# Edge softmax on Trainium2: the second and third bf16 part read as upper halves of fp32 rests, the first part cast by ScalarE

## The reference

```python
w_m = (efeat @ W_msg + b_msg).reshape(E, 16, -1)
w_a = (efeat @ W_attn + b_attn).reshape(E, 16, -1)
h_src = feat[src][:, :, None]
e1 = w_m * h_src
e2 = w_a * h_src
seg_max = jax.ops.segment_max(e2, dst, num_segments=N)
ex = jnp.exp(e2 - seg_max[dst])
denom = jax.ops.segment_sum(ex, dst, num_segments=N)
ft = jax.ops.segment_sum(e1 * (ex / denom[dst]), dst, num_segments=N)
return ft.sum(axis=1)
```

## Time and profile before

| what | before |
|---|---|
| median of three runs | 5007.65 us |
| lowest and highest run | 5004.14 and 5008.03 us |
| the profiled execution | 4998.83 us |
| its span in the profile | 4997.0 us |
| busy in that span: PE, DVE, ACT, POOL | 3246.4, 3526.0, 1651.5, 3172.5 us |
| starts of the softmax's first product (L1403) and last ratio (L1441) | 41.10 and 1365.97 us |
| instructions of the split | 49 of each of the five |

### The profile page before, as it was taken

How to read it: one execution, slowest core, us unless ns; L and a number is a source line. 1 busy time by engine, 2 the same in 40 slices (tenths; PEclk the granted TensorE clock), 3 DMA queues, 4 the chain that set the end, 5 groups by cost and what they waited for, 6 DMA issues and landing times. The chain is left out here.

```text
span 4997.0 us, 55839 instructions
## 1 busy us (share of the span) xinstructions
PE 3246.4 (65%) x12357; PEld 2401.4 (48%) x12357; DVE 3526.0 (71%) x5827; ACT 1651.5 (33%) x4258; POOL 3172.5 (63%) x2763
## 2 busy tenths in 40 slices
PE   7999999999824444427998344453444447777686
PEld 3444444444424444426887334443434326777542
DVE  8999999999976555525888456644556764555688
ACT  4565665666532111103444111131111232222144
POOL 4777777777637888887888777707776007777000
PEclk9999999999976555558999556685566655655698
DMA  4111111111043333432121100040000230000022
GB/s 111 41 44 41 46 44 40 44 45 42 22 127 68 61 59 59 60 37 53 50 54 48 17 7 7 7 110 8 7 7 6 75 81 7 7 7 7 8 66 66
DMA packets 373578, 211.63 MB, mean 42 GB/s; under 512 B 105770, under 2 KB 343662, under 8 KB 373442
## 3 DMA queue, kind: packets, MB, share of 16 engines
q1 hardware_dynamic: 254162, 190.55, 13.3%
q0 software_dynamic: 119296, 19.68, 6.7%
HBM read 151.70 MB, written 58.34 MB: 42 GB/s over the span
## 5 line engine op out<-in xcount | busy, mean ns | idle before, releaser
L697 POOL DMA_INDIRECT extra<-x_t,srci x784 | 763.0, 973 | 503.9 <-issue 490.9
L1161 PE MATMUL ps<-arena 128*128 128x128 f32 x2976 | 662.6, 412 | 635.7 <-DVE arena L1623 583.8
L1161 PEld LDWEIGHTS ps<-arena 128*128 128x128 f32 x2976 | 615.8, 315 | 671.8 <-issue 665.1
L1065 PE MATMUL ps<-edge_in,wl 17*128 17x512 f32 x784 | 701.8, 1072 | 17.6 <-DVE arena L1415 13.5
L684 POOL DMA_INDIRECT sums<-cmb,sidx x392 | 610.9, 1558 | 134.4 <-issue 120.7
L646 POOL DMA_INDIRECT xg<-in_x,xidx x392 | 466.8, 1191 | 259.0 <-DVE xp L1276 139.4
L633 POOL DMA_INDIRECT ft_t<-fts,fidx x392 | 507.3, 1294 | 144.2 <-issue 120.1
L1623 DVE TENSOR_TENSOR arena<-jmask,ps 128x1024 f32<-128x1024 f32 (+1 forms) x186 | 227.0, 1220 | 502.0 <-ACT ps L899 494.9
L1640 DVE TENSOR_TENSOR arena<-arena,ps 128x128 f32 x1488 | 426.1, 286 | 179.9 <-DVE arena L1640 17.3
L697 POOL DMA_INDIRECT extra<-h_t,srci x392 | 369.9, 944 | 241.5 <-issue 241.5
L1104 PE MATMUL ps<-arena 128*128 128x128 f32 x992 | 223.9, 417 | 450.3 <-DVE arena L1491 354.1
(11 more groups left out here) (204 smaller groups left out, 5935.4 us busy)
## 6 DMA issues: line engine op xcount, KB each, us to landing
edge_in<-far_row SPq DMA_DIRECT2D x98, 256.0 KB
ain<-in_src_row SPq DMA_DIRECT2D x56, 448.0 KB, 3.7
sums<-zero SPq DMA_DIRECT2D x132, 144.0 KB, 3.0
arena<-rel_t SPq DMA_DIRECT2D x63, 256.0 KB, 4.0
x_t<-yout SPq DMA_DIRECT2D x28, 448.0 KB, 3.3
xin<-x_t SPq DMA_DIRECT2D x28, 448.0 KB, 4.4
extra<-x_t,srci POOLq DMA_INDIRECT x784, 2.3
ain<-x_t SPq DMA_DIRECT2D x28, 448.0 KB, 4.8
```

The lines of the kernel that those rows point to most:

```text
L697: pool.indirect_dma_start(dy[:, t, :], None, table, bass.IndirectOffsetOnAxis(ap=srci[:, t:t + 1], axis=0)).then_inc(d_gathered[n % QUEUE] ...
L1065: last = pe.matmul(ps[k][:, h * ET:(h + 1) * ET], wl[:, (k * CH + h) * P:(k * CH + h + 1) * P], eft[b][:, :], start=True, stop=True)
L1161: last = pe.matmul(slot_sums(k, n)[:, j * P:(j + 1) * P], oneh[b][:, j * P:(j + 1) * P], placed[b][:, j * P:(j + 1) * P], start=True, stop ...
```

## The change

The two buffers `xp` (bf16 parts) and `xr` (fp32 rests) become one fp32 buffer `xq` with three slots of 16 features per edge. The first part is written by ACT, as a cast of `xg` into the upper halves of slot 0 (new `cast_x`, in every even step behind `copy_xT`, for the pair of tiles n+2 and n+3, and once in the set-up). Slot 1 holds the fp32 rest of `xg` less the first part, and its upper halves are the second part; slot 2 holds the rest of slot 1 less its own upper halves, and its upper halves are the third part. PE reads the upper halves of all three slots: bf16 elements, one every 4 bytes. `split_done` counts two per pair, the new semaphore `x_cast` counts the casts. POOL's next gather waits for the first subtraction of the pair instead of the last cast.

```diff
-        xp = sb("xp", [P, 2 * SUB, PARTS, F], BF16)
-        xr = [sb(f"xr{k}", [P, 2 * SUB, F]) for k in range(2)]
+        xq = sb("xq", [P, 2 * SUB, PARTS, F])
+        high = lambda t: t.bitcast(BF16)[:, 1::2]
+        x_part = lambda a: xq[:, :, a, :].bitcast(BF16)[:, :, 1::2]
...
 (POOL, gather)
                 if later(i, c, 2):
-                    pool.wait_ge(split_done, 5 * nth(i, c))
+                    pool.wait_ge(split_done, 2 * nth(i, c) - 1)
...
 (ACT, step)
                 copy_xT(i, c + 1)
+                if c % 2 == 0:
+                    cast_x(i, c + 2)
...
+            def cast_x(i, c):
+
+                if not inside(i, c, TILES):
+                    return
+                act.wait_ge(x_gathered, 32 * SUB * (nth(i, c) + 1))
+                if later(i, c, 1):
+                    act.wait_ge(xT_ps, 2 * i + c)
+                act.activation(x_part(0), xg[:, :, :], ACT.Copy).then_inc(x_cast, 1)
...
             copy_xidx(0, 2)
+            cast_x(0, 0)
             copy_xT(0, 0)
...
 (PE, transpose)
-                pe.wait_ge(split_done, 5 * (nth(i, c) + 1))
+                pe.wait_ge(split_done, 2 * (nth(i, c) + 1))
...
-                                     xp[:, c % 2 * SUB + k, :, :].rearrange("p a f -> p (a f)"), identb[:, :],
+                                     high(xq[:, c % 2 * SUB + k, :, :].rearrange("p a f -> p (a f)")), identb[:, :],
...
 (DVE, split)
-                part = lambda a: xp[:, :, a, :]
-                dve.wait_ge(x_gathered, 32 * SUB * (n + 1))
-                if later(i, c, 1):
-                    dve.wait_ge(xT_ps, 2 * i + c)
-                dve.tensor_copy(part(0), xg[:, :, :]).then_inc(split_done, 1)
-                dve.wait_ge(split_done, 5 * n + 1)
-                dve.tensor_tensor(xr[0][:, :, :], xg[:, :, :], part(0), ALU.subtract).then_inc(split_done, 1)
-                dve.wait_ge(split_done, 5 * n + 2)
-                dve.tensor_copy(part(1), xr[0][:, :, :]).then_inc(split_done, 1)
-                dve.wait_ge(split_done, 5 * n + 3)
-                dve.tensor_tensor(xr[1][:, :, :], xr[0][:, :, :], part(1), ALU.subtract).then_inc(split_done, 1)
-                dve.wait_ge(split_done, 5 * n + 4)
-                dve.tensor_copy(part(2), xr[1][:, :, :]).then_inc(split_done, 1)
+                rest = lambda a: xq[:, :, a, :]
+                dve.wait_ge(x_cast, n + 1)
+                dve.tensor_tensor(rest(1), xg[:, :, :], x_part(0), ALU.subtract).then_inc(split_done, 1)
+                dve.wait_ge(split_done, 2 * n + 1)
+                dve.tensor_tensor(rest(2), rest(1), x_part(1), ALU.subtract).then_inc(split_done, 1)
```

More of the change, by code:

```diff
@@ L272, in build_program @@
             sem(n) for n in ("p_done", "c_done", "q_done", "den_done", "num_done", "ln_done", "inv_done", "rat_done"))
-        split_done, casts = sem("split_done"), sem("casts")
+        x_cast, split_done, casts = sem("x_cast"), sem("split_done"), sem("casts")
         ft_ps, ft_sb = sem("ft_ps"), sem("ft_sb")
```

## The result

The changed kernel took 4972.81 us in the median of four runs (4970.77 to 4977.85) beside 5007.84 us for the kernel before: a ratio of 0.9934, 95% interval 0.9922 to 0.9945, or 35.0 us less. The forecast was 4971.0, inside a range of 4962 to 4988. The profiled execution of the changed kernel has a span of 4972.7 us, that of before 4997.0.

What follows compares the result with a forecast made beforehand. DVE was taken to bound the edge softmax; 47 splits shorter by 0.78 us each give 36.7 us, with ACT, POOL and PE adding nothing. Off the median of 5007.65 us that forecast 4971.0 us, range 4962 to 4988.

Steps and rivals of the forecast that it cites:

- What bounds the stage: Edge softmax: DVE's own instructions set the pace, busy 194.94 of 200 us; the line beginning a step waited twice in 98.
- The split: DVE, once per pair of steps: three casts and two subtractions become two subtractions, 1.31 to 0.53 us, gain 0.78.
- The number 47: Splits that count in the softmax: 49 less the hidden ones in the set-up and step 1; 36.7 us in all.
- ACT's cast: ACT, one 128x128 cast per pair, 0.27 us, fits in the 1.26 us gap before L758; costed at nothing.
- The cover: ACT's room for the cast: the gap before L758, then 3.3 us more of slack before DVE needs copy L729.
- the mechanism: POOL's next gather, released by the first subtraction, starts earlier against the split; its wait falls from 2.46 to about 1.7 us.
- the rival: POOL takes over: two or three more issues beside DVE's wide scans, 0.9 us each; 5000 to 5008 us, chance 0.05.
- either end of the price: PE's strided bf16 weight load, eight transposes per pair: no change, or 0.55 us more per pair; no cost to the span.
- 0.155 us each: PE's price now per transpose at L1080, from 0.62 / 4; part of 24.80 us of PE work per pair.
- The rival's point of catching up: PE's weight load becomes the bound: it equals DVE at 0.34 us per transpose; at 0.5 us, 5033 us; chance 0.03.
- Half-word reads on DVE: Both subtractions read bf16 at every second place: no extra taken; rival of slow reads, 4978 to 4988 us, chance 0.13.
- The upper end: DVE's strided reads priced from a small stepped copy: 0.18 us extra per subtraction, 16.9 us in all, leaving 19.8 us gain.

Runs made afterwards that it cites:

- The two parts of the change alone: Against the kernel before: only ACT casting the first part, packed (stage 1314.0 us); against the changed kernel: half-word parts with DVE casting the first part (stage 1301.0 us).
- the run with the cast alone: Against the kernel before, ACT casts the first part into the packed bf16 buffer, DVE keeps two subtractions and two casts; stage 1314.0 us.
- twenty casts: Against the changed kernel, twenty more casts into scratch on ACT ahead of the one that counts; stage 1293.8 us, 5.7 longer.
- Five repeats: Against the changed kernel, PE issues the four transpose matmuls of each tile five times; stage 1413.3 us, 125.2 longer.

## Why the prediction was right

**What bounds the stage**: right. Two waits before 98 products, before and after; the stage got shorter by what DVE was spared.

**The split**: forecast 1.31 to 0.53 us, measured 0.53; 0.32 and 0.21 between starts, both as taken. 47 x 0.78 = 36.7 forecast, 36.8 measured. The number 47 is confirmed from the other side, by the wait in step 1 that grew by 0.78. The two parts of the change alone, 10.9 and 23.9 us, bear it out.

**ACT's cast**: forecast 0.27 us long, measured 0.33, hidden as said. The line from 64 to 1024 columns passes below it: the packed cast of the run with the cast alone is 0.296 us in the median. Writing half words adds the rest, 0.335 us, as it does on DVE (0.233 against 0.218). The cover, tried with twenty casts, is at least 4.0 of the 4.3 us read.

**POOL**: the mechanism was right, the size was off. The wait was forecast at about 1.7 us and is 1.34, because the gathers start earlier against DVE's scans and the sixth of them is now 0.3 us longer. This is the contention that the rival named, with a third of an issue where it needed two or three. The rival's time does not follow from its own pairs: 26.7 to 27.6 us are 0.4 to 1.3 above 26.25, which gives 4992 to 5034 us and not 5000 to 5008. The run with the subtractions on POOL, 27.3 us a pair in the mean, took 5019.4.

**PE**: right that nothing was lost, at either end of the price; the weight load at a pitch of 4 bytes costs what the packed one does. The term "0.155 us each" was mis-sized, as was the sum 24.80: it divided and added lengths where only distances between starts add up, the very mistake that the first paragraph on DVE avoids. Measured 0.104 for one more and 24.36. The rival's point of catching up, 0.34 us a transpose, comes out the same (0.104 + 0.235). Five repeats lost 125 us where PE's work alone gives 68, but a part of that is the wait of the `xT` copy whose cause is open, so they do not settle its loss behind that point, one for one with PE's work.

**Half-word reads on DVE**: the lower end was taken, and it was right. The upper end, 0.18 us, was too high even for operands that do jump (0.10).

**The sum**: 4971.0 forecast, 4972.8 and 4972.5 measured. The second is closer than it should be: the kernel before took 5003.37 us beside it, from which the same saving gives 4966.7. The remainder against 36.8 us, 2 to 6 us, lies behind the stage and in the scatter of medians; what makes it is open.

## What to carry to other kernels

Where one engine's instructions stand shoulder to shoulder and the first instruction of its step never waits, an instruction taken off it is worth the distance between starts, times the places where nothing waits behind it; count the places where something does, and leave them out. A bf16 part of an fp32 value need not be cast: its upper half can be read in place, by DVE (0.291 us against 0.293) and by PE's weight load (147 ns against 150), at the price of packed bf16. Before work is moved to another engine, sum that engine's loop by distances between starts with handovers in it, and price the new instruction beside what the other engines do at that time: POOL had 1.04 us of idle in each pair, and the two subtractions took 1.5 us of it in one pair and 4.1 in the next, which cost the changed kernel 47 us.

## What the runs showed of the hardware that was not expected

- PE: a group of four transposes costs 0.58 us between starts, and each further four in the same group only 0.41 to 0.42 (twelve in 1.41, twenty in 2.26 us).
- DVE: element order feature, edge instead of edge, feature on all three operands raises 128 columns from 0.282 to 0.380 us.
- POOL and DVE: two 128x128 subtractions on POOL take 0.63 and 0.40 us, but 1.59 and 2.27 us beside DVE's 1026-wide scans, the second of which then takes 2.49 us instead of 2.27.
- POOL: one indirect gather's issue that takes 0.95 to 1.0 us is 1.82 to 1.88 beside DVE's 1026-wide scans, and 1.34 when it overlaps one in part.
- One chip ran the same programs over a fifth slower. Up to the first gather of the sums by destination (L697) nothing differs, 2754.6 and 2757.1 us in the two profiles of the kernel before; the last one starts at 4619.1 and at 5261.7. The matmuls of these sums (L1161) sat idle for 635.7 us on the one, nearly all for DVE, and for 1454.0 on the other, 952.9 of them with no releaser in the profile. Its cause was not tried.
